# Attention with a mixture of experts on one core: layer normalisations moved to ScalarE, one input load moved forward, and a new order of all jobs

## The reference

```
x = x + attention(layernorm(x))
x = x + experts(layernorm(x))

layernorm(x) = (x - mean) / sqrt(var + 1e-5)          # over the 128 columns
attention:  Q, K, V = silu(x@Wq), silu(x@Wk), silu(x@Wv);  U = x@Wu;  8 heads of 16
            s = (Q K^T + rel_bias[i - j + 255]) / 4, causal, keys whose K row is all zero masked
            out = (silu(s) @ V) * silu(U)             # silu in place of softmax
experts:    logits = x @ w_gate^T; softmax over the best 2 of 8
            y = sum_e gate_e * (x @ w_in[e]^T @ w_out[e]^T)   # 128 -> 512 -> 128, linear
```

## Time and profile before

| | |
|---|---|
| device time, three runs | 326.05, 328.3, 330.67 us; median 328.3 |
| the profiled execution | 330.59 us, of which the span of the trace is 328.4 |
| PE busy | 288.5 us (88%) |
| DVE busy | 244.3 us (74%) |
| ACT busy | 210.9 us (64%) |
| POOL busy | 187.4 us (57%) |
| mean granted PE clock | 0.940 of 2.4 GHz |

### The profile page before, as it was taken

The page is one execution under the profiler, slowest core; times in us unless marked ns, Lnnn a source line. Parts: engine busy times, 40 slices in busy tenths (PEclk is TensorE's granted clock), DMA queues, the critical chain, the costliest instruction groups (busy, mean ns, idle before and its releaser), DMA issues.

```text
span 328.4 us, 5933 instructions
## 1 busy us (share of the span) xinstructions
PE 288.5 (88%) x1860; PEld 136.3 (42%) x1860; DVE 244.3 (74%) x767; ACT 210.9 (64%) x404; POOL 187.4 (57%) x262
## 2 busy tenths in 40 slices
PE   1688998889997999699999989999978999897591
PEld 0535543356444444243344444433434555543240
DVE  4455550672689896699999849789993997698867
ACT  1355464988995788668777868977663688663100
POOL 5293500480016899947953797287664334796672
PEclk9995585999999999999999999999996799999978
DMA  5847895026975916930396000496930010001011
GB/s 172 235 138 192 237 239 168 2 71 198 228 118 154 236 36 192 220 62 3 103 234 142 3 0 1 145 236 198 234 88 2 0 35 0 2 2 32 1 32 32
DMA packets 30669, 36.31 MB, mean 111 GB/s; under 512 B 3240, under 2 KB 17064, under 8 KB 30640
## 3 DMA queue, kind: packets, MB, share of 16 engines
q1 hardware_dynamic: 27232, 33.53, 41.4%
q10 hardware_dynamic: 3408, 2.43, 2.5%
HBM read 23.87 MB, written 12.08 MB: 109 GB/s over the span
## 4 chain that ended last, share of the span: by engine, by line
PE 55%; DVE 23%; POOL 12%; issue 5%; ACT 2%; DMA 2%; SPq 1%; DVEq 0%; POOLq 0%; ACTq 0%
PE o_acc L643 15%; PE score L626 12%; PE jobp L712 12%; DVE score L885 8%; POOL xn L401 8%; PE jobp L676 6%; DVE ymix L986 4%; PE jobp L667 2%; PE jobp L725 2%; POOL rstd L516 2%; PE jobp L684 2%; DMA xs<-in_L_attn_x 2%; PE jobp L705 2%; POOL ymix L572 2%; DVE stats L921 1%
## 5 line engine op out<-in xcount | busy, mean ns | idle before, releaser
L765 ACT ACTIVATE wts<-score 128x512 f32<-128x512 f32 (+2 forms) x200 | 100.6, 531 | 50.4 <-DVE score L885 43.9
L885 DVE TENSOR_TENSOR score<-score,bias_near 128x256 f32<-128x256 f32 (+3 forms) x288 | 113.7, 467 | 24.0 <-PE score L626 23.7
L572 POOL TENSOR_TENSOR ymix<-ymix 128x512 f32<-128x512 f32 (+2 forms) x90 | 74.4, 827 | 41.0 <-DVE ymix L986 35.5
L643 PE MATMUL o_acc<-wts,v_pad 128*32 128x512 f32 (+3 forms) x864 | 83.6, 485 | 1.3 <-ACT wts L765 1.1
L767 ACT ACTIVATE wts<-score,far 128x512 f32<-128x512 f32 x120 | 74.2, 698 | 12.9 <-DVE score L885 5.7
L712 PE MATMUL jobp<-mm_e,xn2T 128*128 128x512 f32 x120 | 66.7, 657 | 5.0 <-DVE ymix L986 3.2
L626 PE MATMUL score<-q_stack,k_stack 64*128 64x256 f32 (+3 forms) x400 | 61.8, 375 | 1.9 <-ACT wts L765 1.7
L626 PEld LDWEIGHTS score<-q_stack,k_stack 64*128 64x128 f32 x400 | 36.1, 191 | 39.5 <-issue 32.9
L986 DVE TENSOR_TENSOR ymix<-jobp,gates 128x512 f32<-128x512 f32 x60 | 40.8, 686 | 14.1 <-PE jobp L712 12.1
L401 POOL TENSOR_SCALAR xn<-xs,mv,rstd 128x128 f32<-128x128 f32 x54 | 42.7, 804 | 1.5
L712 PEld LDWEIGHTS jobp<-mm_e,xn2T 128*128 128x128 f32 x120 | 19.6, 196 | 35.7 <-issue 23.5
(11 more groups left out here) (81 smaller groups left out, 264.0 us busy)
## 6 DMA issues: line engine op xcount, KB each, us to landing
k_stack<-rows_dram SPq DMA_DIRECT2D x32, 256.0 KB, 5.2
q_stack<-rows_dram SPq DMA_DIRECT2D x28, 256.0 KB, 6.6
rows_dram<-k_hi SPq DMA_DIRECT2D x16, 256.0 KB
xs<-in_L_attn_x SPq DMA_DIRECT2D x8, 256.0 KB, 8.9
rows_dram<-k_lo SPq DMA_DIRECT2D x8, 256.0 KB
rows_dram<-q_hi SPq DMA_DIRECT2D x7, 256.0 KB
rows_dram<-q_lo SPq DMA_DIRECT2D x7, 256.0 KB
out<-xs SPq DMA_DIRECT2D x7, 256.0 KB, 7.5
```

Source lines behind the costliest of these rows:

```text
L572: then_wait(pool.tensor_tensor(y[:, 0:n], y[:, 0:n], y[:, n:2 * n], ALU.add))
L643: ins = pe.matmul(o_acc[32 * j:32 * j + 32, q0:q0 + n], v_pad[:, b % 2, kb, 4 * quad + j, :], wts[:, group % WTS, j, c:c + n], start=USES[ ...
L765: act.activation(weights, score[bank][:, 0:n], ACT.Silu, scale=HD ** -0.5).then_inc(weighed[bank], 1)
L885: ins = dve.tensor_tensor(score[bank][:, c + near:c + n], score[bank][:, c + near:c + n], bias, ALU.add)
```

## The change

1. The normalisation is no longer done by POOL or DVE but by ACT at the places norm1 and norm2: one activation per tile, Identity(rstd * x + shift), with both factors as per-partition operands. POOL computes shift = -mean * rstd with two more small instructions in `scale`, and its wait for the earlier normalisation moves there from DVE.
2. The second half of x is loaded ahead of expert 0.
3. BEFORE is one list, and almost every job has another place in the lists.

```diff
@@ loads at the start
             sp.dma_start(rb_s[:], rel_bias[MAXLEN - 1:, :].rearrange("(p t) h -> p t h", p=P)).then_inc(rb_in, 16)
+            load_x(0, 1)
             load_expert(0)
-            load_x(0, 1)
@@ POOL, scale
                 pool.wait_ge(averaged, n + 1)
+                if b > 0:
+
+                    pool.wait_ge((normed1, normed2)[ln], 1 + (unit_before(args[0]) if ln else 2 * (b - 1) + args[1]))
                 then_wait(pool.tensor_tensor(rstd[:, ln, ts], mv[:, ln, ts, 1], eps_t[:, ts], ALU.add))
-                pool.tensor_tensor(rstd[:, ln, ts], rstd[:, ln, ts], mhalf[:, ts], ALU.pow).then_inc(scaled, 1)
-                if not norm_on_dve((("norm1", "norm2")[ln],) + args):
-                    pool.wait_ge(scaled, n + 1)
-                    normalise(pool, args, ln)
+                pool.tensor_tensor(shift[:, ln, ts], mv[:, ln, ts, 0], minus[:, ts], ALU.mult)
+                then_wait(pool.tensor_tensor(rstd[:, ln, ts], rstd[:, ln, ts], mhalf[:, ts], ALU.pow))
+                pool.tensor_tensor(shift[:, ln, ts], shift[:, ln, ts], rstd[:, ln, ts], ALU.mult).then_inc(scaled, 1)
@@ ACT, jobs
+                if kind in ("norm1", "norm2"):
+                    ln = int(kind == "norm2")
+                    b, tiles = rows_of(args, ln)
+                    act.wait_ge(scaled, SCALES.index((args, ln)) + 1)
+                    if b > 0:
+
+                        wait_filled(act, ("T2", unit_before(args[0])) if ln else ("T1", b - 1, args[1]))
+                    for t in tiles:
+                        ins = act.activation((xn1, xn2)[ln][:, t], xs[:, b, t], ACT.Identity,
+                                             bias=shift[:, ln, t:t + 1], scale=rstd[:, ln, t:t + 1])
+                    ins.then_inc((normed1, normed2)[ln], 1)
@@ DVE, stats
-                        dve.wait_ge((normed1, normed2)[ln], 1 + (unit_before(args[0]) if ln else 2 * (b - 1) + args[1]))
+                        dve.wait_ge(scaled, SCALES.index(((unit_before(args[0]),) if ln else (b - 1, args[1]), ln)) + 1)
@@ BEFORE
-    [],
-    [("stats1", 0, 0), ("RB",), ("T1", 0, 0), ("stats1", 0, 1), ("norm1", 0, 0), ("WT", 0), ("K", 0, 0),
-     ("V", 0, 0), ("split", 0, 0), ("MASK", 0, 0), ("Q", 0, 0), ("norm1", 0, 1), ("U", 0, 0)],
-    [("T1", 0, 1), ("norm1", 1, 0), ("WT", 1), ("Q", 0, 1), ("REL",), ("norm2", 0), ("K", 0, 1), ("split", 0, 1)],
+    [("stats1", 0, 0), ("RB",), ("stats1", 0, 1), ("norm1", 0, 0), ("T1", 0, 0), ("WT", 0), ("norm1", 0, 1),
+     ("K", 0, 0), ("V", 0, 0), ("T1", 0, 1), ("U", 0, 0), ("Q", 0, 0), ("Q", 0, 1), ("split", 0, 0), ("K", 0, 1),
+     ("MASK", 0, 0), ("REL",)],
```

## The result

The changed kernel takes **305.28 us** (median of four runs, 303.84 to 307.0) against 327.45 us (326.05 to 330.67) for the kernel before: a ratio of 0.931 [0.9225, 0.9399]. The direction was forecast, the size was not: 319.3 us, range 309 to 331. The gain is 22 us and not 9. The profiled execution took 303.84 us, of which 302.1 are span, 26.3 less than before. It is the fastest of its four, and that of the kernel before (330.59 us) is 3 us above its median, so a lead read from the two profiles is larger than the typical one.

What follows compares the result with a forecast made beforehand. PE was taken as the bound (busy 288.5 of 328.4 us), so only its idle time and clock could move. The terms +3 - 5 - 3 - 3 + 1 - 2 = -9 us took 328.3 to 319.3 us, range 309 to 331.

Steps and rivals of the forecast that it cites:

- the sum's only term for the clock: Near 250 us: the low clock vanishes if PE's wait before it does, -3 us, bounds 0 and -5.7.
- the third rival: Early steps: half clock shrinks by some 20 us because prologue projections stand in one block; 10 us more gain, 309 us; chance 0.11.
- The tail: After the last product with V: -7.6 there, +5.3 for jobs moved ahead, together -2 us, bounds -6 and +1.
- PE's waits for the normalisation: Ahead of the transposes: most of 9.9 us goes but DVE is late next, -5 us, bounds 0 and -9.9.
- ACT in steps 7 to 19: From 57.1 to 102.0 us: ACT paces and gets 3.8 us more work, +3 us, bounds 0 and +7.
- The first rival: Whole kernel: ACT's 26.8 us more work holds back PE and takes the gain, -2, 326 us; chance 0.28.
- The prologue: Kernel start: earlier x and first scores near 19.6, against later stack loads, -3 us, bounds -5 and -1.
- The expert loads: Expert 7's load has 4.5 to 6 us before WT 7 instead of seven steps: +1 us, bounds 0 and +6.
- the half clock: Rival for steps 7 to 19: PE gaps where ACT paces keep the clock low, +17, 336 us; chance 0.09.
- one table load: Rival at the norm jobs: Identity needs another table, two loads per job, 44 us more, 363 us; chance 0.02.
- The signs named for the forecast: POOL about 150 us, Identity 0.45-0.55, ACT 235-240, normalisation wait below 4, first scores 19-20.5, tail 18-20, no low clock near 250.
- One sign against it: Whole kernel: the prediction is wrong if ACT's waits for POOL's factors add up to several us.

Runs made afterwards that it cites:

- e3: Kernel before plus two useless 128x512 products on PE ahead of the scores of group 1: 323.98 us, ratio 0.984.
- e4: Changed kernel plus a PE wait, ahead of the scores of group 1, until POOL has finished the relative bias: 310.44 us.
- e2: Changed kernel with new places and load order, but the normalisation back on POOL, and on DVE for the first batch and unit 8: 312.63 us.
- e5: Kernel before with its old places and loads, but all normalisations on ACT: 316.85 us.
- e8: Kernel before with the new prologue alone (second half of x early), other places and normalisation as before: 326.69 us.
- e6: Changed kernel with four FF halves of batch 3 moved back from entries 75 and 76 into the tail: 309.33 us, ratio 0.934.
- e7: Changed kernel with split 0 1 moved from entry 0 back to the end of the prologue: 301.43 us, ratio 0.914.
- e1: Changed kernel with the second half of x loaded behind expert 0 again: 304.29 us, ratio 0.923.
- e11: Changed kernel with split 0 1 at the end of the prologue and the second half of x behind expert 0 again: 300.63 us.

## Why the prediction was right or wrong

**The clock was one mis-sized term.** The step that failed is the sum's only term for the clock, "it vanishes if the wait before it does: -3 us". The low clock at 250 did vanish, as forecast. But the early low clock stood in the sum at nothing, and it went too; I had left that to the third rival with a chance of 0.11, by the argument that only its coming right after a PE wait spoke for it. Across the 36 executions of the kernel before that were timed beside the experiments, the span follows 315.0 + 0.345 x the us of low clock (twice the missing share of the mean clock, times the span), with a correlation of 0.948, from 321.1 us at 0.971 to 332.8 at 0.924; chip by chip the factor is 0.26 to 0.40. The profiled executions have 2 x 0.060 x 328.4 = 39 us of it before and 2 x 0.013 x 302.1 = 8 after; 31 x 0.345 makes -11 instead of -3. On average it is 34 us in those 36 executions and 10 in ten of the changed kernel, which makes -8. Of the kernel before's early low clock (23.9 us by the windows; the 28 us of the prediction came from the rounded-down digits) 3.4 us are left.

That PE's idle time in the first steps brings low clock, and that low clock costs this much, is shown from both sides: e3 takes it away with work (median of the mean clocks 0.970 against 0.950), e4 brings it back with a wait (0.972 against 0.984). What lifted it in the changed kernel stays open: both halves of the change do it in their profiled executions (e2, e5), the new prologue alone doesn't (e8), and the same 0.65 us of idle time is followed by a fall in some executions and not in others. So the third rival was right about the clock, and its cause, "the projections of the prologue stand in one block", is refuted as sufficient by e8, which has that block and keeps the low clock. The Trainium skill (TensorE: Matmul & The Clock Gate, Part 1) has the lower clock as the default that activity lifts. The mean clocks of e3 and e4 agree; the fall at 46.7 us before, behind 18 us in which PE shows no idle time, says that the busy share of this view does not tell whether that activity is enough.

**The tail was the other.** The forecast was -7.6 + 5.3 = -2 us. The tail gave -8.7 (18.3 forecast for it, 17.2 measured). The other half failed: "costing PE 4 x 1.1 + 0.9 = 5.3 us there". By e6 the four halves (4.4 us by that price, T2 and LOG weren't tried) cost 1.2. They add eight products and 1.6 us of PE's busy time (18.52 against 16.91): steps that the view shows as over 90% busy had room for this work at three quarters off. Why it fits in so cheaply isn't shown; the ends of the recorded products are modelled, so a high busy share doesn't say that PE is full. Groups 72 to 79 got shorter in spite of them, 19.55 instead of 23.71 us, because other jobs had left: PE has 176 instructions there instead of 186, DVE 50 instead of 63 and 15.2 us of work instead of 19.6.

**PE's waits for the normalisation** were forecast at -5 of 9.9 us. Behind the prologue 1.0 us is left, so -9, near the bound. The engine wasn't what did it: in e2 0.8 us of them is left with POOL still normalising, in e5 6.1 us with ACT.

**ACT in steps 7 to 19** was forecast at +3. The stretch from group 6 to 19 didn't change (38.98 and 39.05); the move of the engine costs 0.4 there by e2. ACT is busy for 97% of it, as the list said, but went from 35.1 to 37.7 and not up by the 3.8 forecast, and the stretch had that room. The reading "PE can't use the room, because ACT paces" isn't borne out: with 3.3 us less on ACT, e2 is 0.4 shorter there. The first rival, that ACT takes the gain, is refuted: e2, which keeps the normalisation away from ACT, is 7 us slower. (Its price was also added up wrong: with +4 for ACT, +5 for the expert loads and +3 for the waits it is 331 us and not 326.)

**The prologue** was forecast at -3. The first scores came at 19.01 (19.6 forecast), -3.7; the stack loads were 2.65 us late (0 to 1 forecast), and e7, which removes that wait, is 3.9 us faster. The load of x is worth 1.0 us at group 0 and nothing that shows at the end (e1).

**The expert loads** cost nothing (+1 forecast): between 49 and 93 us PE's list of waits has no load in it, only DVE's key mask with 1.2 us, ACT's normalisation with 1.0, and two smaller.

The sum of the terms as measured: clock -11, waits -9, first scores -3.7, stacks +2.65, FF beside +1.2, ACT +0.4, tail -8.7, together -28. The span fell by 26.3, and by the table 8.3 us of that come up to group 0, 10.6 between groups 19 and 79 and 8.7 in the tail, with 1.3 lost between groups 0 and 19. The terms aren't independent (a wait that goes takes its low clock with it), so 2 us of overlap are no surprise, but they are not assigned.

Of the other rivals, the half clock did not stay, and there is one table load, as before. The signs named for the forecast hold for POOL (150.0), the Identity, the first scores, the wait (1.0 us behind the prologue, 4.5 with it) and the clock at 250; ACT's busy time was 230.7 instead of 235 to 240, and the tail one us better. One sign against it was met in form: ACT's waits for POOL's factors add up to 7.8 us. But 2.8 of them lie ahead of the first normalisation and 4.6 ahead of the last one, in the tail, and only 0.4 between, so they say little of the steps for which the sign was meant.

**Left open:** why the same kernel keeps the clock in one execution and not in the next (e5, e7, e11), which of the changes lifted the early clock, and by how much each single job's place counts among those of the new lists.

## What to carry to other kernels

Before pricing a change by its waits, look at where the clock falls in the profile before, and give each such stretch a term of its own in the sum: where PE is the bound a us of low clock was worth about a third of a us here, and idle PE in the first steps cost once as a wait and once as clock. Time several executions before you call a clock gained, since the same kernel keeps it in one and loses it in the next. A job moved out of the tail, where it delays the end by its whole length or more, cost a fifth of that beside other work, even in steps that showed PE busy for over 90%. Two cures for the same wait can't both be paid in full by it: price the second on top of the first.

## What the hardware showed that was not expected

- With a single product of 1.13 us more at 20 us, six of six executions kept a mean clock of 0.992 or more; without it two of six fell to 0.970 (303.7 instead of 298.6 us of span), and two of six in e11 to 0.966 and 0.970. Six executions make it likely, not certain, that the product does it.
- The clock fell to half at 46.7 us in the kernel before while PE's timeline had no idle time for the 18 us ahead, and it stayed up in after behind 0.65 us of idle time that was followed by a fall in e1, e6 and e8.
- DVE's cast of K (128x512) took 0.418 us in the median and 1.373 at the longest before (mean 0.563); after, the longest is 0.553 (mean 0.435). POOL's normalisations aren't the reason: in e5, where POOL has none, the longest is 1.198 (mean 0.539), and beside a normalisation before (at 120 us) the cast took 0.418. The two longest stand beside POOL's subtraction q_lo (at 23.5 us before, 22.6 us in e5). The Trainium skill (SBUF — State Buffer, SBUF: two separate sides) says that GpSimd and VectorE can block each other at a shared port. The casts beside q_lo fit that; the one beside the normalisation shows no delay, and no run here separates it from other causes.
